# A wait put between the second and third gather of each tile: a two-layer kernel of deformable sampling on one core

## The reference

```python
x = x + _L0_conv_ref(_gn(x), ...)   # K = 4 learned sampling points for each pixel, bilinear,
                                    # softmax weights, 1x1 projection, batch norm, gelu
x = x + _L1_conv_ref(_gn(x), ...)   # below
...
offset = _conv2d(x, w_p, b_p, padding=1)               # 2 x 9 offsets for each pixel
m = jax.nn.sigmoid(_conv2d(x, w_m, b_m, padding=1))    # 9 modulations
p = offset + p_0[None] + p_n[None, :, None, None]      # 9 sampling positions for each pixel
...
x_off = g_lt[:, None] * gather(q_lt_x, q_lt_y) + g_rb[:, None] * gather(q_rb_x, q_rb_y) \
      + g_lb[:, None] * gather(q_lt_x, q_rb_y) + g_rt[:, None] * gather(q_rb_x, q_lt_y)
x_off = x_off * m                                      # 9 bilinear samples x 32 channels for each pixel
return _conv2d(x_off, w_conv, None, stride=KS)         # sum over 9 samples and 32 channels
```

## Time and profile before

| | us |
|---|---|
| median of 3 runs | 536.71 |
| lowest and highest | 532.47, 537.18 |
| span of the profiled execution | 702.7 |
| TensorE busy in it | 543.3 (77%) |
| VectorE busy | 392.4 (56%) |
| GpSimd busy | 326.1 (46%) |
| ScalarE busy | 147.7 (21%) |

### The profile page before, as it was taken

How to read it: one execution, slowest core, us unless ns; L and a number is a source line. 1 busy time by engine, 2 the same in 40 slices (tenths; PEclk the granted TensorE clock), 3 DMA queues, 4 the chain that set the end, 5 groups by cost and what they waited for, 6 DMA issues and landing times.

```text
span 702.7 us, 10708 instructions
## 1 busy us (share of the span) xinstructions
PE 543.3 (77%) x3862; PEld 294.6 (42%) x3862; DVE 392.4 (56%) x876; ACT 147.7 (21%) x292; POOL 326.1 (46%) x336
## 2 busy tenths in 40 slices
PE   4838898794853788868888788887878888776777
PEld 3515555563721334333444333343434334433344
DVE  3346768684444655556555455665555666544564
ACT  3202211112520221222222121222112122121201
POOL 2363656520053555544555544455554455455440
PEclk9999999997695899997899988899898879889869
DMA  4995787830580111111211361111111111111110
GB/s 111 276 210 128 159 169 123 144 69 3 166 222 27 36 50 43 51 52 44 66 50 54 72 80 37 31 39 40 40 42 35 34 35 38 38 38 42 33 35 11
DMA packets 41924, 52.24 MB, mean 74 GB/s; under 512 B 16766, under 2 KB 32930, under 8 KB 41872
## 3 DMA queue, kind: packets, MB, share of 16 engines
q1 hardware_dynamic: 31464, 30.19, 19.9%
q0 software_dynamic: 10240, 20.99, 11.2%
q10 hardware_dynamic: 168, 0.34, 0.2%
HBM read 34.80 MB, written 8.72 MB: 62 GB/s over the span
## 4 chain that ended last, share of the span: by engine, by line
PE 53%; another core or an unknown queue 17%; DVE 12%; issue 12%; DMA 2%; ACT 2%; DVEq 1%; SPq 0%; POOL 0%; ACTq 0%
PE ps_later L1178 9%; PE ps_pair L1178 8%; PE ps_raw L980 5%; PE ps_x L1191 5%; PE ps_raw L1152 3%; DVE vprod L1620 3%; PE ps_x L1045 3%; PE ps_x L1201 3%; DVE vlast L1620 2%; PE ps_o L993 2%; PE ps_later L1023 2%; PE ps_pair L1045 1%; DVE prod L1819 1%; DMA shared<-positions 1%
## 5 line engine op out<-in xcount | busy, mean ns | idle before, releaser
L614 POOL DMA_INDIRECT got<-table,idx x320 | 318.8, 996 | 296.6 <-DVE prod L1819 147.6
L1620 DVE TENSOR_TENSOR vprod<-ps_pair,rhat 128x704 f32<-128x704 f32 x64 | 57.0, 890 | 71.6 <-remote 31.4
L1620 DVE TENSOR_TENSOR vprod<-ps_later,rhat 128x704 f32<-128x704 f32 x64 | 56.7, 885 | 42.1 <-PE ps_pair L1178 25.3
L1191 PEld LDWEIGHTS ps_x<-early,vprod 128*128 128x128 f32 x384 | 49.8, 163 | 42.4 <-issue 33.6
L1191 PE MATMUL ps_x<-early,vprod 128*128 128x128 f32 x384 | 65.4, 315 | 0.6 <-DVE vlast L1631 0.6
L1178 PE MATMUL ps_later<-columns_of,shared 64*64 64x352 f32 x320 | 43.6, 554 | 19.5 <-DVE vlast L1620 11.3
L1178 PE MATMUL ps_pair<-columns_of 64*64 64x352 f32 x320 | 41.9, 557 | 20.6 <-DVE vlast L1620 10.3
L1802 DVE TENSOR_TENSOR samples<-shared,vprod 128x800 f32<-128x800 f32 x48 | 47.1, 986 | 11.9 <-PE ps_x L1045 4.8
L1628 DVE TENSOR_TENSOR vprod<-vprod 128x640 f32<-128x640 f32 x64 | 52.5, 821 | 1.2
L1152 PE MATMUL ps_raw<-conv_out,later 128*128 128x512 f32 x64 | 44.5, 780 | 10.9 <-issue 10.2
L1178 PE MATMUL ps_pair<-columns_of,shared 64*64 64x352 f32 x320 | 39.5, 526 | 15.2 <-DVE vlast L1620 5.9
(11 more groups left out here) (216 smaller groups left out, 722.9 us busy)
## 6 DMA issues: line engine op xcount, KB each, us to landing
shared<-positions SPq DMA_DIRECT2D x24, 440.0 KB
xn<-xq SPq DMA_DIRECT2D x52, 132.0 KB, 3.9
got<-table,idx POOLq DMA_INDIRECT x320
table<-trow SPq DMA_DIRECT2D x9, 234.0 KB
table<-trow SPq DMA_DIRECT2D x2, 1024.0 KB, 4.5
out<-ysumT SPq DMA_DIRECT2D x64, 16.0 KB
columns_of<-table SPq DMA_DIRECT2D x2, 512.0 KB
table<-trow SPq DMA_DIRECT2D x1, 936.0 KB
```

The costliest lines, as they stand in the source:

```text
L614: pool.indirect_dma_start(into[t][:, s * P:(s + 1) * P], None, tab, bass.IndirectOffsetOnAxis(ap=idx[:, slot, k:k + 1], axis=0),).then_inc ...
L1191: nc.tensor.matmul(bank[:, P:2 * P], vprod[:, t % 2, r, :], idn[:], start=(r == 0), stop=(r == HALF - 1), is_transpose=True)
L1620: nc.vector.tensor_tensor(dst, ps_dense[pair_number(0, t, pair) % 2][:].rearrange("p (d n) -> p d n", d=2)[:, :, 0:WROWS * C].rearrange("p ...
```

## The change

In the second layer GpSimd waits once more for each tile, between its second and third gather (60 of the 64 tiles; group 0 has no such wait). It waits until VectorE has read pair 0 and pair 1 of the tile that follows the one whose buffer is being filled again: for tile t of group g that is tile t + 1 of group g - 1, and for t = 3 it is tile 0 of group g. A `sem_inc` of the semaphore `slot_taken`, for which nobody waits, stands behind the wait, as it does behind the wait for `used`. The first layer and the branch for far offsets call `gather` without `pause` and are unchanged.

```diff
-            def gather(tab, S, slot, t, done, into=got):
+            def gather(tab, S, slot, t, done, into=got, pause=None):
                 for s in range(S):
                     k = t * S + s
+                    if pause is not None and s == S // 2:
+                        pool.wait_ge(*pause)
+                        pool.sem_inc(slot_taken, 1)
                     pool.indirect_dma_start(into[t][:, s * P:(s + 1) * P], None, tab,
                                             bass.IndirectOffsetOnAxis(ap=idx[:, slot, k:k + 1], axis=0),
                                             ).then_inc(done, 16)
...
                 for t in range(TT):
                     pool.wait_ge(used, (NGA + g) * TT + t + 1)
                     pool.sem_inc(slot_taken, 1)
-                    gather(table[1][b], GT, u, t, arrived[1][t])
+                    first = isinstance(g, int) and g == 0
+                    after = pair_number(g - 1, t + 1, 1) if t + 1 < TT else pair_number(g, 0, 1)
+                    gather(table[1][b], GT, u, t, arrived[1][t], pause=None if first else (v_read, after + 1))
```

## The result

| | before | changed |
|---|---|---|
| median of 20 runs each, us | 538.26 | 538.52 |
| lowest, highest | 532.47, 543.95 | 535.55, 542.57 |
| ratio, changed to before | | 1.0052, 95% interval 1.0028 to 1.0077 |
| span of the profiled execution | 702.7 | 534.6 |

The forecast of 536.9 us stood on a base of 536.71 us from 3 runs; with 20 runs the base itself is at 538.26. The two medians are 0.3 us apart; the ratio says +0.5%. Both lie inside the 1% that I had set as "same".

What follows compares the result with a forecast made beforehand. GpSimd's gathers were taken to bound the second layer, 5.2 us a tile, with TensorE close behind or even. The change's terms summed to 0, +1.0 us at most: 536.7 + 0.2 = 536.9 us; range 526 to 549.

Steps and rivals of the forecast that it cites:

- The bound: Second layer, timed runs: GpSimd's gathers follow one another nearly without a gap, 5.2 us a tile, TensorE close behind or even.
- The first sum: Whole kernel: the profiled span less GpSimd's waits for VectorE, 702.7 - 147.6 - 19.0 = 536.1 us.
- Step 1: GpSimd's queue, second layer: the added wait, when already met, and its `sem_inc` cost 0 us.
- Rival B: Slower: the restart is paid before each third gather, 29 us, 566 us (551 if TensorE is even); chance 0.10.
- Step 2: New wait: never held if GpSimd is last; if ahead, 69 us of the 147.6 change releaser, none of it new.
- a second releaser, L1620, with some 30 waits and about 70 us: Sign in the profile after: GpSimd's waits get this releaser, and those for L1819 fall by as much.
- L1819 keeps its idle time of 0: Sign in the profile after: VectorE's `weigh_corners` still never waits for gathered data.
- Step 3: After a held wait, GpSimd falls behind by 1.0 us at most, once, not adding up over tiles.
- Step 4: Third and fourth gather still land in time for VectorE's weighing: with 5 us for landing, some 7.8 us are left.
- Step 5: Shifted gathers meeting VectorE operations: no new lengthened ones, or 15 us more at worst, 17 us less at best; taken as 0.
- rival C: Slower: held pauses put the third gather onto L1628 or L1819 in tiles with two pairs, 15 us, 552 us; chance 0.08.
- Rival A: Faster: gather bursts hold the other engines up and a pause in mid-burst shortens that, 520 us; chance 0.16.

Runs made afterwards that it cites:

- run 1: The kernel before, unchanged, timed against itself and profiled a second time: 539.03 against 539.47 us, ratio 0.9957.
- run 4: The kernel before with three of the four gathers issued for each tile of the second layer: 511.79 us, ratio 0.9512.
- run 2: The changed kernel, unchanged, timed and profiled once more: 539.60 us, ratio 1.0002.
- run 3: The changed kernel with the added wait's threshold one group earlier, so that it is always met: 540.56 us, ratio 0.9986.
- run 5: The changed kernel, all four gathers, with the pause waiting for the weighing of the next tile instead of its two reads: 539.20 us, ratio 0.9957.
- run 6: The changed kernel, all four gathers, with the pause waiting for the weighing of the tile two further on: 538.23 us, ratio 0.9977.
- run 8: Three gathers a tile as in run 4, plus a pause before the third until the weighing of the next tile: 511.06 us, ratio 0.9489.
- run 7: The changed kernel, all four gathers, with the pause waiting for the weighing of the tile three further on: 572.46 us, ratio 1.0591.

## Why the prediction was right

**The bound (5.2 us a tile on GpSimd, estimated from a trace that did not show it).** Right in the bound, and helped by luck in the sums. They gave 536.1 and 535.8 us; the second profile of before has a span of 533.5, and 335.2 us for 64 tiles, 5.24 each. The layer itself was put at 333 and took 335. But two of my terms were off and cancelled: the second layer begins at 188.4 us and not 179.3, and the tail is 9.9 us and not 23.5. I had taken out the first layer's 19.0 us of waits for L1810 as if they belonged to that execution; run 1's profile has 19.2 us of them, so they are the kernel's own. And I had left in a first layer and a tail that were stretched in that execution. The first sum has the same two errors. "I can't tell which of the two is last" is settled by run 4: GpSimd is, with 27.7 us before TensorE would be. My 5.4 us a tile for TensorE was too high: with three gathers the weighings L1819 come 4.7 us apart (200.47 to 497.35 us for 63 tiles).

**Step 1, the instructions cost 0.** Right, by the sum of the gaps (78.1, 78.0, 78.1, 78.0 us in runs 1, after, 2 and 3) and by run 3. The row that I had used, the boundary between two tiles in a burst, was the same pair of instructions, and it held. Rival B fell with it.

**Step 2, when the wait is met.** For the timed kernel right: never held. The 0.7 and 3.9 us that I had worked out for the long execution say nothing of the timed one, and I expected them in the profile after ("a second releaser, L1620, with some 30 waits and about 70 us"). There were 12 with 3.6 us, all of the usual gap. "L1819 keeps its idle time of 0" failed too: 41.3 us. Both failed for one reason, that I let the profile after follow the trace and not the sum in which I believed for the time.

**Step 3, at most 1.0 us, once.** Not tested, since nothing was held. No run here holds a wait on `v_read`: all pauses that were held waited on `used`. Runs 5 and 6 show that there is more room than it needed: a threshold up to two tiles later changes nothing that can be measured.

**Step 4, the data is in time.** Right for a GpSimd that is ahead, by run 8, where the pauses are held and the time stays. The landing was set at 5 us and is about 1.6 us in most tiles of run 1. Run 7 gives the limit: with half a tile of lead the price is 5.9%.

**Step 5, lengthened gathers.** Right at 0. Above 0.944 us each, the second layer's gathers carry 15.4 us in the second profile of before, 15.0 and 16.0 in the two of the changed kernel, 15.3 in run 3. I had worked out 13 us for this term. Of the 15.4 us, gathers that start inside an L1628 carry 10.5, those inside an L1819 carry 2.8 and nine that start with an L1587 carry 2.0; all three operations read two inputs in SBUF. The 60 gathers that start inside an L1620 reading `ps_pair`, which is in PSUM, carry 0.1 together. The lengthening is what is left of the VectorE operation less 0.12 us, as for the two gathers in rows 3 and 4 (0.63 us left, 0.51 longer; 0.31 left, 0.19 longer); most gathers that start within 0.04 us of the start of the operation aren't lengthened. The trace agrees with the rule of the Trainium skill ("SBUF — State Buffer", section "Who interferes with whom") that such a DVE instruction contends with a GpSimd instruction that reads SBUF. So L1628, only the second candidate in (5), is the main one. Nothing of it was changed here, and rival C had no place.

**Rival A (the bursts hold the other engines up).** Not borne out. Run 8 splits the bursts of run 4 differently and gains nothing (0.9489 and 0.9512, intervals that overlap), and in the profiles at normal length GpSimd issues 256 gathers without a break while TensorE is busy for 170.5 of 180 us at the full granted clock:

```profile
300.00:480.00 180.00, 170.47 (x1610) 86.60 (x1609) 148.45 (x322) 55.13 (x115) 137.98 (x138) 1.00 0.26 63
```

(the window 300 to 480 us of run 1; columns as in the earlier trace rows). What held all engines up in the one execution with 702.7 us stays open. Its page puts 17% of the chain that ended last down to an unknown queue and none to GpSimd, which has 23% in run 1:

```profile
PE 53%; another core or an unknown queue 17%; DVE 12%; issue 12%; DMA 2%; ACT 2%; DVEq 1%; SPq 0%; POOL 0%; ACTq 0%
```

The granted clock in its second layer was 0.85, against 0.97 in run 1. It did not come again in nine further profiles, one of them of the same kernel, and no experiment was aimed at it.

## What to carry to other kernels

A wait costs what it holds, and it holds nothing on an engine that is already behind it. Before pricing an added wait, find how far the waiting engine runs behind its threshold; here that was 5 to 15 us, and only the threshold that left half a tile was felt. When a profile's span is far from the measured time, take its waits out and see whether one engine's work alone adds up to the measured time: then that engine is the bound, and the waits in the trace belong to that execution. A second profile tells which do: of those that I took out here, 19 us were the kernel's own. And time a kernel against itself before believing half a per cent.

## What the runs showed of the hardware

One profiled execution took 702.7 us where nine others of this kernel and its variants with four or three gathers took 506 to 576 us. In it VectorE and ScalarE had idle times of several us with an unknown releaser, in step with GpSimd's bursts; no timed run shows such a length.

In the second layer's 255 gaps of run 1, of the changed kernel and of runs 2 and 3, GpSimd's gap between two indirect DMAs is 0.30 to 0.32 us whether nothing, or a wait that is met and a `sem_inc`, stands between them. After a wait on `used` that is not met the next one starts 0.77 to 0.80 us after the end of the operation that releases it (69 of 70 such waits in runs 4, 7 and 8, one at 0.99).

An indirect DMA of 0.94 us that starts inside a VectorE operation with two SBUF inputs was up to 0.65 us longer, by what was left of that operation less 0.12 us, but mostly not where the two started within 0.04 us of each other (run 1, the changed kernel, runs 2 and 3).
